# A build-time walk that tries each choice of TensorE in a two-layer attention kernel

## The chip, the cores and the metric

The kernel runs on one core of a Trainium2 chip. The metric is the device time of one execution in microseconds; the time of a version is the median of its runs. A core has five engines that run side by side and meet through semaphores: PE (TensorE; its weight loads are listed as PEld), DVE (VectorE), ACT (ScalarE), POOL (GpSimd) and SP (SyncE, which only issues DMAs here).

## The reference

For each of 16 images of 64 channels by 56 x 56 tokens there are two layers. Layer 0 is windowed cosine attention (8 heads of 8 channels, windows of 7 x 7 tokens) with a group norm, an MLP and a second residual. Layer 1 is full attention over all 3136 tokens:

```
h = _window_cosine_attn(x, qkv_w, qkv_b, logit_scale, bias_table, rel_index, proj_w, proj_b)
h = jax.nn.relu(_group_norm(x + h, gn1_w, gn1_b, GROUPS))
m = _group_norm(h, mlp_gn_w, mlp_gn_b, GROUPS)
m = jax.nn.relu(jnp.einsum('bchw,ec->behw', m, mlp_w1) + mlp_b1[None, :, None, None])
m = jnp.einsum('behw,ce->bchw', m, mlp_w2) + mlp_b2[None, :, None, None]
z = jax.nn.relu(_group_norm(h + m, gn2_w, gn2_b, GROUPS))
...
attn = jax.nn.softmax(jnp.einsum('bhdn,bhdm->bhnm', q, k) * scale, axis=-1)
out = jnp.einsum('bhnm,bhdm->bhdn', attn, v).reshape(b, c, h, w)
return jnp.einsum('oc,bchw->bohw', w_proj, out) + x
```

In layer 1 there are 4 heads of 16 channels. Its softmax subtracts the true maximum of each row, so every score is computed twice: once for the maxima and once for the exponentials.

## The kernel before

**Layer 1 as steps.** An image's attention is 8 stages: 4 heads times 2 halves of the queries. A stage is 25 tiles of 128 keys, and a tile is 4 units of 392 queries, so there are 800 units u = 0 to 799 per image. Unit u has `score` u (one matmul of 392 columns into one of three PSUM banks), then `exp` u on ACT into one of eight buffers, and each fourth unit is followed by `weigh` q, which multiplies the four exponentials of tile q by V in four 32-column tiles of the array. `score` u waits for `exp` u - 3. A `max` step is two matmuls on PE and one maximum over them on DVE; there are 400 per image, 200 for each two heads, and those of a stage must be finished before the stage begins. A `shift` step then moves the negated maxima into three rows of `q_stack` through SP. `copy` and `store` take a stage's result to DRAM.

**Layer 0 as steps.** During the attention of image b the kernel also computes layer 0 of image b + 1: `xload` and `xorder` (x from DRAM, reordered by windows on POOL), `qk`, `sum`, `norms`, `spread`, per window row g the steps `wscore`, `wsum`, `wval`, `wtrans`, `wpv`, `wproj`, then the group norms (`gn`, `affine`, `relu`, `zrelu`), `mlp1` and `mlp2`, and last `gqk`, `gv` and the twelve transfers of each `stack`, which put Q and K of the next image in place. `stack` 3 of an image is issued in the next loop iteration, since head 3 is in use until then. Each half of an image is ended by `sums` (row sums from DRAM), `zload`, `srecip` (DVE), `rden`, `rspread`, `scale` (POOL), `final` (PE and DVE) and `write`.

**Two PSUM slots.** All steps of the list `SLOTS`, that is all but `score` and `weigh`, take turns on two slots of two banks; such a step waits on PE until the one two places before it is emptied by DVE or ACT. DVE, ACT, POOL and SP each take their instructions in program order, so an instruction that waits holds back all behind it.

**The order is written at build time.** `arrange` walks through one image with a clock of its own, in units of 10 ns: `PARTS` is how long each part of a step takes on its engine, `TAIL` how long until others may use it. The engine that is free first takes the offered step of lowest rank. `MORE` is the order of the loop's 15 iterations, `LAST` that of the sixteenth image (no layer 0 beside it), `PROLOGUE` is layer 0 of the first image and `EPILOGUE` the last half's end. These costs only set the order; nothing on the chip waits for them. Three lines on SP matter below; the third is the first thing that `sums` does:

```
                        sp.wait_ge(s_out_copied, b * STAGES + 1)
...
                        sp.wait_ge(s_x_by_windows, t * 8 + g - 1)
...
                    sp.wait_ge(s_out_stored, b * 512 + (64 if half == 1 else 512))
```

The first belongs to `stack` 3, the second to `xload` g from g = 2 on: x_in has two buffers, and POOL must have reordered the earlier one.

## Time and profile before

| | |
|---|---|
| median of 3 runs | 10851.35 us (10829.22 to 10851.8) |
| the profiled execution, its own time | 10812.4 us |
| its span in the trace | 10810.6 us |
| mean granted clock of TensorE | 0.95 |
| PE busy | 9939.2 us (92%) |
| DVE busy | 7775.1 us (72%) |
| ACT busy | 6386.1 us (59%) |

A share of busy time is a mean over the whole span. An idle stretch is listed in the trace in brackets behind the instruction that ended it, with the engine and line that released it. The granted clock has two levels here, 1.2 GHz (0.5) and 2.4 GHz (1.0), so a stretch's mean says what part of it was spent at the lower one.

### The profile page before, as it was taken

The numbers are of one execution on the slowest core, as the hardware profiler recorded it, in microseconds if no ns is written. First come the engines' busy times: TensorE is split into PE (matmuls) and PEld (weight loads), VectorE is DVE, ScalarE is ACT, GpSimd is POOL, SyncE is SP. The second block draws the span as 40 slices with busy tenths as digits, with TensorE's granted clock in tenths as the row PEclk, the third lists the DMA queues.
The fourth block names the chain that finished last, engine by engine and source line by source line (L and its number), as shares of the span: only waits on it lengthen the run. The fifth ranks groups of instructions, "written<-read, shape, count | busy, mean of one in ns | idle before, by whom it ended". The sixth has DMA issues, their size and how long they took to land.

```text
span 10810.6 us, 221389 instructions
## 1 busy us (share of the span) xinstructions
PE 9939.2 (92%) x69254; PEld 3841.5 (36%) x69254; DVE 7775.1 (72%) x10052; ACT 6386.1 (59%) x14066; POOL 972.7 (9%) x834
## 2 busy tenths in 40 slices
PE   5899999999999999999999999999999999999998
PEld 2333433334333333333333333343333433333332
DVE  4676877768677786776767777687776867778675
ACT  1365665656656566565656656566565665656666
POOL 3100101001010000100001010110100101000000
PEclk8799999999999999999999999999999999999999
DMA  0202011020110201111020110201102011020100
GB/s 22 34 5 38 10 19 26 8 36 8 24 22 13 32 7 25 21 20 25 6 33 14 19 25 6 39 8 19 26 8 37 8 25 20 12 33 7 25 14 15
DMA packets 109028, 213.92 MB, mean 20 GB/s; under 512 B 52854, under 2 KB 84534, under 8 KB 107706
## 3 DMA queue, kind: packets, MB, share of 16 engines
q1 hardware_dynamic: 107842, 198.78, 11.5%
q8 instruction: 663, 10.86, 0.4%
q14 instruction: 523, 4.28, 0.1%
HBM read 66.03 MB, written 41.47 MB: 10 GB/s over the span
## 4 chain that ended last, share of the span: by engine, by line
PE 74%; DVE 6%; ACT 6%; DMA 6%; issue 4%; SPq 3%; POOL 1%; ACTq 0%; DVEq 0%; POOLq 0%
PE PS L1219 21%; PE PS L1074 19%; PE PS L1208 16%; DVE small L860 4%; PE PS L1115 3%; ACT exps L796 3%; PE PS L1133 2%; PE PS L1163 2%; PE PS L1171 2%; DMA x_in<-in_x 2%; DMA scratch_rden<-small 2%; PE PS L1123 2%; SPq L592 1%; PE PS L1197 1%; PE PS L1179 1%
## 5 line engine op out<-in xcount | busy, mean ns | idle before, releaser
L796 ACT ACTIVATE exps<-PS 128x392 f32<-128x392 f32 x12800 | 5475.9, 500 | 3683.6 <-PE PS L1208 3655.9
L860 DVE TENSOR_REDUCE small<-PS 128x1 f32<-128x784 f32 x6400 | 5970.6, 968 | 1777.1 <-PE PS L1074 1751.1
L1208 PE MATMUL PS<-q_stack,k_stack 99*128 99x392 bf16 x12800 | 3426.2, 341 | 201.6 <-ACT exps L796 196.3
L1074 PE MATMUL PS<-k_stack,q_stack 96*128 96x392 bf16 x12800 | 3202.9, 342 | 317.0 <-DVE small L860 202.6
L1219 PE MATMUL PS<-exps,v_all 128*32 128x392 f32 x25600 | 2870.8, 521 | 11.9 <-ACT exps L796 9.4
L1208 PEld LDWEIGHTS PS<-q_stack,k_stack 99*128 99x128 bf16 x12800 | 1241.4, 99 | 2077.3 <-ACT exps L796 1156.9
L1074 PEld LDWEIGHTS PS<-k_stack,q_stack 96*128 96x128 bf16 x12800 | 957.5, 99 | 2650.5 <-issue 1217.8
L1219 PEld LDWEIGHTS PS<-exps,v_all 128*32 128x32 f32 x25600 | 510.9, 109 | 800.9 <-issue 582.9
L695 POOL TENSOR_TENSOR win_scores<-win_scores,small 128x784 f32<-128x784 f32 x256 | 383.9, 1500 | 3424.6 <-DVE small L910 3424.6
L1115 PE MATMUL PS<-kmask,tok_unit 113*64 113x392 f32 (+1 forms) x2048 | 398.6, 510 | 33.2 <-DVE small L860 21.3
L753 ACT ACTIVATE win_probs_t<-PS 98x1024 f32<-98x1024 f32 x256 | 262.1, 1024 | 169.7 <-PE PS L1133 167.8
L898 DVE TENSOR_REDUCE small<-PS 128x16 f32<-128x784 f32 x256 | 248.2, 970 | 145.2 <-PE PS L1115 145.2
L1133 PE MATMUL PS<-ident_f,win_scores 128*98 128x128 f32 x2048 | 283.3, 283 | 27.0 <-DVE small L860 21.3
L708 POOL TENSOR_TENSOR att<-att,inv_sums 64x784 f32<-64x784 f32 x66 | 119.8, 1833 | 1814.0 <-DMA inv_sums<-scratch_rden 1814.0
L901 DVE TENSOR_TENSOR win_scores<-PS,small 128x784 f32<-128x784 f32 x256 | 249.5, 975 | 36.8 <-DVE small L898 7.4
L1133 PEld LDWEIGHTS PS<-ident_f,win_scores 128*98 128x98 f32 x2048 | 220.6, 130 | 146.9 <-DVE small L860 124.1
L1197 PE MATMUL PS<-att,w_p 64*64 64x392 f32 x264 | 141.1, 671 | 120.0 <-POOL att L708 120.0
L909 DVE TENSOR_REDUCE small<-win_scores 128x16 f32<-128x784 f32 x256 | 244.5, 955 | 8.8 <-ACT win_scores L748 8.8
L773 ACT ACTIVATE win_scores<-PS,vec 128x392 f32<-128x392 f32 x256 | 136.5, 584 | 192.3 <-PE PS L1163 192.3
L748 ACT ACTIVATE win_scores<-win_scores 128x784 f32<-128x784 f32 x256 | 221.7, 866 | 39.4 <-DVE win_scores L901 38.0
L983 DVE TENSOR_TENSOR inv_sums<-PS,z_half 64x392 f32<-64x392 f32 x132 | 68.0, 552 | 230.4 <-PE PS L1197 230.4
L1123 PE MATMUL PS<-w_v,x_tw 64*98 64x64 f32 x2048 | 208.7, 253 | 9.1 <-DVE win_scores L901 9.1
(102 smaller groups left out, 4151.6 us busy)
## 6 DMA issues: line engine op xcount, KB each, us to landing
q_stack<-tok_qk SPq DMA_DIRECT2D x320, 98.0 KB, 3.7
k_stack<-tok_qk SPq DMA_DIRECT2D x320, 98.0 KB, 4.2
kmask<-tok_unit SPq DMA_DIRECT2D x1024, 12.2 KB
scratch_att<-o_st SPq DMA_DIRECT2D x512, 26.0 KB
att<-scratch_att SPq DMA_DIRECT2D x33, 392.0 KB
z_half<-scratch_z SPq DMA_DIRECT2D x33, 392.0 KB, 11.1
inv_sums<-scratch_rden SPq DMA_DIRECT2D x132, 98.0 KB, 3.3
out<-inv_sums SPq DMA_DIRECT2D x33, 392.0 KB, 3.7
```

The lines of the kernel that those rows point to most:

```text
L695: nc.gpsimd.tensor_tensor(S3, S3, rden[:, 16 * half:16 * half + 16].unsqueeze(2) .broadcast_to([128, 16, WTOK]), ALU.mult).then_inc(s_win_ ...
L753: nc.scalar.activation(win_probs_t[0:2 * WTOK, 2 * half:2 * half + 2, :], PS[0:2 * WTOK, it.bank:it.bank + 2, :], ACT.Copy)\
L796: nc.scalar.activation(exps(u), PS[:, u % SCORE_BANKS, 0:GTOK], ACT.Exp, scale=D1 ** -0.5).then_inc(s_exps, 1)
L860: nc.vector.tensor_reduce(max_parts[:, n_:n_ + 1], slot(), op=ALU.max, axis=AX.XY)\
L901: nc.vector.tensor_tensor(pair(win_scores, half).rearrange("p (a h m) -> p a h m", a=2, m=WTOK), scores, top.unsqueeze(3).broadcast_to([12 ...
L1074: last = mm(PS[:, it.bank + j, 0:GTOK], q_stack[0:STACK, stage // 2, tile * 128:(tile + 1) * 128], k_stack[0:STACK, stage // 2, chunk * GT ...
L1115: last = mm(PS[64 * (w % 2):64 * (w % 2) + m, it.bank + i // 2, 0:GTOK], tok_unit[0:CH + WTOK, q0:q0 + m], kmask[0:CH + WTOK, :, w * WTOK: ...
L1123: last = mm(PS[0:2 * WTOK, it.bank, w * CH:(w + 1) * CH], x_tw[:, w, :, :].rearrange("c a m -> c (a m)"), w_v0[:], start=True, stop=True)
L1133: last = nc.tensor.transpose(PS[0:2 * WTOK, it.bank + p, q * 128:(q + 1) * 128], win_scores[:, c0:c0 + 2 * WTOK], ident_f32[:])
L1197: last = mm(PS[0:CH, it.bank + j, 0:GTOK], w_p1[:], att[:, sl], start=True, stop=True)
L1208: mm(PS[:, u % SCORE_BANKS, 0:GTOK], k_stack[0:STACK + SHIFT, h, kt * 128:(kt + 1) * 128], q_stack[0:STACK + SHIFT, h, c * GTOK:(c + 1) * ...
L1219: last = mm(PS[32 * j:32 * j + 32, PV_BANK, 0:GTOK], v_all[:, stage // 2, kt, :], exps(4 * quad + j), start=(kt == 0), stop=(kt == TILES - 1))
```

## The change

The build-time walk becomes a class `Walk`. Where PE has more than one step to choose from, `arrange` copies the walk, takes one candidate of each kind (`score`, `weigh`, `max`, "layer 0"), runs the copy on for `AHEAD` = 600 units (6 us of the walk's own clock) and keeps the candidate after which PE got most work done. `weigh` has no fixed place among the scores any more: it must only keep its own order, and jumps ahead once 7 scores are out beyond it. `SWITCH` adds 9 units where PE goes from an ordinary step to one in array tiles or back, and the tiled steps' own costs are lowered. `LATE` replaces one constant by a table of how late transfers are counted. `stack` 3 now asks for `sums` 1 first, so it stands behind it on SP. In `earliest_unit`, layer 0's window rows stand 13 quads apart instead of 10, and `final` has no earliest place. No instruction of any engine differs but in its place, apart from the waits on registers that a merged row needs or not.

```
-    "score": (("PE", 17),), "exp": (("ACT", 41),), "weigh": (("PE", 86),),
+    "score": (("PE", 17),), "exp": (("ACT", 41),), "weigh": (("PE", 69),),
...
-STACK_TAIL = 900
+LATE = {"stack": 1200, "xload": 800, "sums": 1500, "zload": 1500, "rden": 600, "rspread": 700}
+AHEAD, PATIENCE = 600, 40
+SWITCH, TILED, URGENT = 9, ("weigh", "sum", "wscore", "wpv"), 7
...
-MAX_START, MAX_RATE = 1, 2.0
+MAX_LOW, MAX_START, MAX_RATE = 4, 6, 2.0
...
-    needs[at("stack", 3)] = []
+    needs[at("stack", 3)] = [(at("sums", 1), None)]
...
-    first, period = 20, 10
+    first, period = 18, 13
...
-    for k in range(2):
-        quad[at("final", 1, k)], quad[at("final", 0, k)] = 8 + k, 185 + k
...
+                behind = self.taken < MAX_LOW + MAX_RATE * self.unit / 4
+                overdue = self.unit > self.pace[n] + PATIENCE if self.pace[n] else False
+                rank = {"shift": 0, "max": 1 if behind else 3}.get(kind, 0 if overdue else 2)
...
+            elif e == 0:
+                if step.i != self.weighed:
+                    continue
+                rank = 0 if self.scored - 4 * self.weighed >= URGENT else 5
...
+        if e == 0:
+            duration += SWITCH * (self.tiled != (kind in TILED))
+            self.tiled = kind in TILED
...
+        if e == 0 and len(found) > 1 and found[0][0]:
+            tried, firsts, until = [], {}, walk.free[0] + AHEAD
+            for _, _, n in found:
+                kind = walk.tasks[n][0].kind
+                firsts.setdefault(kind if kind in ("score", "weigh", "max") or not attended else "layer 0", n)
+            for m, n in enumerate(firsts.values()):
+                other = walk.again()
+                other.take(0, n)
+                tried.append((-min(walk.took[n], AHEAD) - other.work(until), m, n))
+            best = min(tried)[2]
```

The first place is SP at the start of a loop iteration. Before, the twelve transfers of `stack` 3 stand first (`q_stack<-` and `k_stack<-`), then `sums` (`small<-scratch_att` and `att<-`), `zload` and the x loads:

```order
L592 DMA q_stack<-tok_qk 16x3136 x5
L592 DMA q_stack<-piece_l 16x3136
L592 DMA k_stack<-tok_qk 16x3136 x4
L592 DMA k_stack<-piece_l 16x3136
L592 DMA k_stack<-tok_qk 16x3136
L603 ISA
L478 ISA
L605 DMA small<-scratch_att 128x1x49
L607 DMA att<-scratch_att 64x1x1568
```

With the change the same place has `sums`, `zload`, the first four x loads, then `stack` 3, and `rden` (`scratch_rden<-small`) behind it:

```order
L643 DMA x_in<-in_x 64x392
L669 ISA
L677 DMA q_stack<-tok_qk 16x3136 x5
L677 DMA q_stack<-piece_l 16x3136
L677 DMA k_stack<-tok_qk 16x3136 x4
L677 DMA k_stack<-piece_l 16x3136
L677 DMA k_stack<-tok_qk 16x3136
L702 ISA
L703 DMA scratch_rden<-small 128x49
```

So `sums` moved ahead of the twelve stack transfers, and those moved behind the fourth x load, which waits for POOL.

The second place is PE in the same stretch, at the first steps of layer 0. Before, at unit 28, `qk` 1 (`PS<-x_w,w_qk`) is followed by a maximum, two scores and a `weigh` (the ISA rows are its waits):

```order
L1084 ISA
L1060 ISA
L1088 MATMUL PS<-x_w,w_qk 128x392 x2
L1060 ISA
L1074 MATMUL PS<-k_stack,q_stack 128x392 x2
L1207 ISA
L1208 MATMUL PS<-q_stack,k_stack 128x392
L1207 ISA
L1208 MATMUL PS<-q_stack,k_stack 128x392
L1217 ISA
L1219 MATMUL PS<-exps,v_all 32x392 x4
```

With the change `qk` 0, 1 and 2 stand in a row at unit 43:

```order
L1173 MATMUL PS<-x_w,w_qk 128x392 x2
L1169 ISA
L1145 ISA
L1173 MATMUL PS<-x_w,w_qk 128x392 x2
L1169 ISA
L1145 ISA
L1173 MATMUL PS<-x_w,w_qk 128x392 x2
L1292 ISA
L1293 MATMUL PS<-q_stack,k_stack 128x392
```

So the first three `qk` steps have moved from units 24, 28 and 32 to unit 43 and stand next to each other; the two `final` steps follow at unit 47 instead of 32 and 37. On DVE, `srecip` 1 now stands behind sixteen `max` steps of the iteration instead of six. Late in the image `final` 0 moved from units 740 and 745 to 772.

The third place is PE in the steady part of the sixteenth image, where scores (`PS<-q_stack,k_stack`), maxima (`PS<-k_stack,q_stack`) and `weigh` (`PS<-exps,v_all`) are all that is left. Before:

```order
L1219 MATMUL PS<-exps,v_all 32x392 x4
L1074 MATMUL PS<-k_stack,q_stack 128x392 x2
L1208 MATMUL PS<-q_stack,k_stack 128x392 x2
L1074 MATMUL PS<-k_stack,q_stack 128x392 x2
L1208 MATMUL PS<-q_stack,k_stack 128x392 x2
L1219 MATMUL PS<-exps,v_all 32x392 x4
```

With the change:

```order
L1304 MATMUL PS<-exps,v_all 32x392 x4
L1293 MATMUL PS<-q_stack,k_stack 128x392
L1159 MATMUL PS<-k_stack,q_stack 128x392 x2
L1293 MATMUL PS<-q_stack,k_stack 128x392 x2
L1159 MATMUL PS<-k_stack,q_stack 128x392 x2
L1293 MATMUL PS<-q_stack,k_stack 128x392
L1304 MATMUL PS<-exps,v_all 32x392 x4
```

The same work stands between two `weigh` steps, but one score has moved from before a `weigh` to behind it.

## Rows read from the trace of the kernel before

**Rows 1.** The page's part 1: busy time and instructions of each engine

```profile
PE 9939.2 (92%) x69254; PEld 3841.5 (36%) x69254; DVE 7775.1 (72%) x10052; ACT 6386.1 (59%) x14066; POOL 972.7 (9%) x834
```

**Rows 2.** One DVE line of layer 0, once per image (count, first and last start)

```profile
L881 DVE TENSOR_SCALAR tok_h<-PS x15: 566/567/567, 429.6 to 9670.6; 128x392 f32<-128x392 f32 x15
```

**Rows 3.** Windows of one image: length, busy (x instructions) by engine, then PEclk, DMA, GB/s

```profile
3012.00:3069.00 57.00, 46.91 (x224) 15.96 (x221) 31.17 (x36) 22.86 (x49) 14.40 (x15) 0.78 0.43 67
...
3109.00:3149.00 40.00, 38.79 (x334) 17.37 (x327) 31.13 (x38) 26.68 (x58) 5.24 (x4) 1.00 0.05 11
...
3563.00:3594.00 31.00, 30.50 (x211) 11.02 (x209) 25.52 (x34) 21.71 (x52) 0.00 (x0) 1.00 0.01 2
3594.00:3636.00 42.00, 35.89 (x215) 12.09 (x214) 26.46 (x32) 22.07 (x52) 3.62 (x2) 0.88 0.23 43
```

**Rows 4.** Timeline of DVE and PE at an image's start: start, length, [idle before <-releaser]

```profile
3026.03 0.47 DVE L975 RECIPROCAL small<-small 128x49 f32<-128x49 f32 x1 [6.64 <-DMA small<-scratch_att]
...
3027.38 0.83 PE L1074 MATMUL PS<-k_stack,q_stack 96*128 96x392 bf16 x2 [5.66 <-DVE small L860]
...
3038.21 1.58 PE L1088 MATMUL PS<-x_w,w_qk 64*128 64x392 f32 x4 [2.57 <-POOL x_w L673]
```

**Rows 5.** Timeline of SP, same stretch: start and length of issuing

```profile
3008.77 1.26 SPq L544 DMA_DIRECT2D scratch_att<-o_st  x4
...
3023.04 0.61 SPq L605 DMA_DIRECT2D small<-scratch_att  x1
...
3025.79 13.23 SPq L558 DMA_DIRECT2D x_in<-in_x  x4
3039.15 0.51 SPq L618 DMA_DIRECT2D scratch_rden<-small  x1
...
3042.41 1.88 SPq L624 DMA_DIRECT2D inv_sums<-scratch_rden  x4
```

**Rows 6.** Timeline of POOL, same stretch

```profile
3037.07 1.01 POOL L673 COPY x_w<-x_in 64x392 f32<-64x392 f32 x2 [27.67 <-DMA x_in<-in_x]
...
3047.68 3.66 POOL L708 TENSOR_TENSOR att<-att,inv_sums 64x784 f32<-64x784 f32 x2 [2.53 <-DMA inv_sums<-scratch_rden]
```

**Rows 7.** Timeline at the same image's end: SP, then PE

```profile
3594.15 1.25 SPq L544 DMA_DIRECT2D scratch_att<-o_st  x4
3601.21 0.58 SPq L605 DMA_DIRECT2D small<-scratch_att  x1
...
3604.13 0.36 SPq L618 DMA_DIRECT2D scratch_rden<-small  x1
3614.40 1.70 SPq L624 DMA_DIRECT2D inv_sums<-scratch_rden  x4
...
3621.35 2.84 PE L1197 MATMUL PS<-att,w_p 64*64 64x392 f32 x4 [6.07 <-POOL att L708]
```

**Rows 8.** Timeline of PE with four scores, a maximum and a weigh

```profile
2494.21 0.66 PE L1208 MATMUL PS<-q_stack,k_stack 99*128 99x392 bf16 x3
...
2495.13 0.34 PE L1208 MATMUL PS<-q_stack,k_stack 99*128 99x392 bf16 x1
2495.40 0.87 PE L1219 MATMUL PS<-exps,v_all 128*32 128x392 f32 x8
2496.20 0.84 PE L1074 MATMUL PS<-k_stack,q_stack 96*128 96x392 bf16 x4
```

**Rows 9.** Timeline of SP: the first and last issue of two stacks

```profile
3498.36 3.39 SPq L592 DMA_DIRECT2D q_stack<-tok_qk  x5
...
3517.97 0.94 SPq L592 DMA_DIRECT2D k_stack<-tok_qk  x1
```

**Rows 10.** The sixteenth image on PE: at its start and at its last final

```profile
10292.10 0.83 PE L1074 MATMUL PS<-k_stack,q_stack 96*128 96x392 bf16 x2 [8.20 <-DVE small L860]
...
10737.21 5.46 PE L1197 MATMUL PS<-att,w_p 64*64 64x392 f32 x8 [6.39 <-POOL att L708]
```

**Rows 11.** Waits over the whole span: total us, times, longest

```profile
PE PS L1074 <- DVE small L860: 202.6, 325, 8.2
```

More of the change, by code:

```diff
@@ L242, in arrange @@
                 if kind == "max":
[L243 removed]
+                    if self.maxima[self.taken] != step[1:]:
                         continue
[L245 removed]
+                    if self.unit < UNITS - 1 and self.taken > MAX_START + MAX_RATE * self.unit / 4:
                         continue
[L247 to L253 removed]
```

199 lines of the change are left out of this document (124 added, 75 removed).

## The prediction

> **What bounds the kernel now.** I read the page's busy times first. PE is busy for 92% of the span, DVE for 72%, ACT for 59% [rows 1], so the question is how PE's time is filled, and only waits that end on PE count. The second view is one line of layer 0 that runs once per image: its 15 starts lie 14 images apart, (9670.6 - 429.6) / 14 = 660.1 us per image [rows 2]. The third is a table of windows of one image, cut where 50 more units are scored; the table has 16 windows, four are shown [rows 3]. An even window, 3109 to 3149, is 40 us long with 38.8 us of PE at clock 1.00. Two stand out. The first, 3012 to 3069, is 57 us long at a granted clock of 0.78: its 46.9 us of PE would be 46.9 x 0.78 = 36.6 us at the full clock. The other, 3594 to 3636, is 42 us at 0.88, so 35.9 x 0.88 = 31.6 us of work, where the window before it took 31 us. Then I read the timelines of these two for the wait that starts each.
>
> At the start DVE stands 6.64 us at the reciprocal of the row sums until their transfer lands, and PE waits 5.66 us for the maximum behind it; eleven microseconds later PE waits 2.57 us for POOL, which waits for x [rows 4]. SP had sent the twelve transfers of `stack` 3 ahead, so the sums left only at 3023.04 and the first x load at 3025.79 [rows 5]. At the end PE waits 6.07 us for POOL's scaling: SP sent the sums 7.1 us after the store, `rden` needed 10.3 us until 3614.40, and PE could begin 7.0 us after that [rows 7]. After each such wait the clock is at its lower level for a while: 2 x (1 - 0.78) x 57 = 25 us of the first window, 2 x 0.12 x 42 = 10 us of the other [rows 3].
>
> The third thing to see is small and everywhere. Three scores, a maximum and a fourth score: the fourth starts 0.92 us after the first, where the work between is 3 x 0.165 + 0.33 = 0.83 us or less; with four scores in a row it would be 0.50 us [rows 8]. The fourth needs the bank that the exponential of the first empties, so 0.92 us is the least distance of `score` u from u - 3.
>
> **The change part by part.** The work stays: the same matmuls, maxima and exponentials. Everything is a move.
>
> *Start of an image.* The sums cannot leave before the last store has landed. It was issued at 3008.77 [rows 5], and 7.06 us pass at the other such place [rows 7]: 3015.8 instead of 3023.0. `srecip` stands ten maxima later on DVE, at unit 21, some 15 us on, so the 5.66 us go. What is late next is layer 0. The first x load follows the sums by 2.75 us, at 3018.6; before, 11.3 us passed from its issue to POOL's reorder, which takes 1.0 us for two [rows 5, 6], so both are ordered at 3030.9. Only then may SP send the next two x loads and `stack` 3 behind them, 10.3 us of issues (two stacks in 20.5 us [rows 9]), so `rden` leaves at 3042 and x 4 and x 5 a microsecond later. With `rden`'s own 3.3 us [rows 5] as a price for them too, x 5 is ordered at 3047. PE comes to `qk` 0 at unit 43: of the 36.6 us for 50 units [rows 3] I take off seven layer-0 or `final` steps of about 1.5 us (one of them took 1.58 [rows 4]), add five more maxima at 0.34 and take 43/50 of it, 23.9 us, 24.6 with the even window's 3%; 3 us more, my estimate, for the lower clock at the image's start. That is 3039.7. `qk` 0 and 1 fit, `qk` 2 waits from 3042.8 to 3047, 4.3 us. `rspread` goes out 3.3 us after `rden`, scaling starts 5.3 us later and its first half is done after 1.8 us [rows 5, 6]: 3052.4, where PE arrives at 3051. So 8.2 us of wait become about 6, and one spell of low clock of two goes. At half speed, 10 us of it cost 4.5 us. Gain 2.5 + 4.5, and something for `final`: **8 us**. Bounds: 57 - 36.6 x 40 / 38.8 = **19 us** if no wait is left; **3 us** if the moved `stack` 3 delays `qk` 2 and `final` by 5 us more.
>
> A rule bears on this. The row shows 11.3 us for a load of 98 KB [rows 5, 6]. The Trainium skill (DMA: Bandwidth & Descriptors, section on queues, rings and completion order) says that each DMA engine consumes descriptors in ring order. By that the load stands behind `att` and `z_half`, which still precede it, and the 11.3 us stay; if they came from the stack's transfers instead, x 0 would be ready some 8 us sooner and `qk` 2 would hardly wait, 4 us more gain per image. I take the slower reading.
>
> *End of an image.* `final` 0 moves from units 740 and 745 to 772. The sums leave at about unit 711 as before, `srecip` now stands at unit 738, and from `rden` to PE it took 17.2 us [rows 7]. The window 3563 to 3594 had 31 us for 50 units [rows 3], so the 34 units to 772 are 21 us: no wait, by 4 us. The window falls from 42 to 31.6 x 31 / 30.5 = 32 us at best, 10 us; I take **8 us**, bounds 0 and 10.
>
> *Spacing of scores.* Matmuls of scores and maxima start 0.165 us apart: three take 0.66 us and four 0.84 us, the last one's own 0.34 among them; so `score` is 0.165 and `max`, two of them, 0.33. `weigh` to the next start is 0.80, and a score before it 0.27, that is 0.10 more [rows 8]. With these I counted in both orders the scores that stand less than 0.92 us behind the third one before. In `MORE` 131 are short by 21.6 us together, with the change 71 by 8.7 us. In `LAST` it is 197 by 28.3 us and then 50 by 14.5 us. Some of it lies in stretches that wait anyway. **12 us** per image, bounds 6 and 13.
>
> *Waits for maxima elsewhere.* 202.6 us over the span [rows 11], less 5.66 x 15 + 8.2 for the starts, is 109 us or 7 us per image. The walk that looks ahead sees them; new rows of eight `mlp` steps may make others. **3 us**, bounds -4 and 7.
>
> *Switches.* Each costs the 0.10 us above. The order has 417 switches between ordinary and tiled steps, with the change 413: nothing. The Trainium skill (TensorEngine Tiling (Array Packing), section Key Properties) says that a change of tiling mode drains the engine; by it too the sum would move only by these four. This speaks against the weights of the change, not for them.
>
> *The sixteenth image.* Its start wait of 8.20 us goes with 2 us of clock, 10 us; the wait of 6.39 us before the last `final`, whose 8 matmuls ran at half speed [rows 10], goes too, 9 us; spacing 13 us. **32 us**.
>
> Sum: 15 x (8 + 8 + 12 + 3) + 32 = 497 us. From the profiled execution's 10812.4 that is 10315; the median of the runs shown is 39 us above it, so the forecast is **10350 us**, 4.6% faster.
>
> **Rivals.**
> 1. *Waits are truly gone.* The x loads come early and `qk` 2 does not wait: 11 us more per image, 10350 - 165 = 10185. For it: DMA is only partly busy there (0.43 [rows 3]). Against: the 13.2 us that four x loads held SP [rows 5].
> 2. *Half is given back.* PE's waits move to `qk` 2 and `final` 1 (3 us gain at the start), scores stand further apart but then wait for an ACT that is behind after the four `relu` in a row (2 us), maxima nothing: 15 x 13 + 20 = 215, 10635.
> 3. *Nothing changes*: PE's busy 92% is the bound and moved gaps only merge. The clock of 0.78 beside a wait speaks against. 10850.
> 4. *Slower, by one mechanism.* Layer 0 ends about 80 units later, so `stack` 0 to 2 are issued from unit 630 on, and `shift` 7 stands behind all three on SP. Three stacks take 31 us [rows 9]; with 0.62 us per unit [rows 3] they end near unit 675, and the shift is due at 700, 15 us later. Each microsecond beyond is a wait of all of PE. It decides when the stacks end 15 + 31 = 46 us late; at 50 us late it costs 35 per image against 31 won: 10350 + 15 x 35 = 10875, and the low clock behind such a wait (10 us of it, 4.5 us each) makes it 10940.
>
> **How the numbers follow.** My forecast, 10220 to 10480 from start gains of 3 to 15 and the other bounds: 0.50. Rival 1: 0.17. Rival 2: 0.18. Rival 3: 0.05. Rival 4: 0.10. The range 10180 to 10640 reaches from rival 1 to rival 2. The runs shown differ by 0.2%, which is about what a measurement can tell from no change. Faster by over 0.2%: 0.86 (the first three, and a tenth of rival 4), within: 0.05, slower: 0.09.
>
> **What the next profile would show.** Right: no DVE reciprocal behind idle time at an image's start; a PE wait of some 4 us at `qk` 2 and a smaller one at `final` 1; `final` 0 without one; the clock near 0.85 in the first window and 1.00 in the last; the period of the layer-0 line near 629 us. Wrong: a PE wait of over 10 us at `qk` or `final` 1, a `shift` 7 that lands after its stage is due, or a period with the waits gone and still over 645 us, which would mean that PE's own work was longer than I priced it.

## The result, and the profile after

| | before | after |
|---|---|---|
| median of the runs | 10840.28 us (4 runs, 10785.34 to 10851.8) | 10125.55 us (4 runs, 10120.28 to 10143.26) |
| profiled execution, its span | 10812.4 us, 10810.6 us | 10121.69 us, 10119.9 us |
| mean granted clock | 0.950 | 0.968 |

The ratio is 0.9354, 95% interval 0.9327 to 0.938: 6.5% faster. The forecast was 10350 us with a range down to 10180, so the direction is right and the time lies below the range. The spans differ by 690.7 us, where 497 were forecast.

The page after, busy times first (busy us, share of the span, instructions), then the chain that ended last by engine:

```profile
PE 9685.7 (96%) x69254; PEld 3807.6 (38%) x69254; DVE 7762.6 (77%) x10052; ACT 6507.8 (64%) x14066; POOL 974.3 (10%) x834
...
PE 83%; DVE 5%; DMA 4%; SPq 3%; issue 2%; ACT 2%; POOL 1%; DVEq 0%; ACTq 0%; POOLq 0%
```

The instructions are the same in number, and DVE's busy time with them [rows 1]. PE's busy time fell by 253 us although its work stayed: busy time is not work, since a matmul at the lower clock lasts nearly twice as long (eight of one `final` took 5.46 us in [rows 10] and take 2.84 us at the full clock, below).

The line of layer 0 that [rows 2] count, from the second image's call on (count, shortest/median/longest ns, first and last start):

```profile
L966 DVE TENSOR_SCALAR tok_h<-PS x14: 565/566/568, 1040.7 to 9070.6; 128x392 f32<-128x392 f32 x14
```

(9070.6 - 1040.7) / 13 = 617.7 us per image, against 660.1: 42.4 us, where the four terms add up to 31.

Windows of the fifth image, units 0 to 50, 50 to 100, 700 to 750 and 750 to the next image (columns as in [rows 3]); the last line is the same stretch before, units 750 to the next image:

```profile
2832.00:2881.00 49.00, 45.92 (x220) 16.05 (x218) 33.53 (x39) 21.51 (x49) 12.88 (x14) 0.81 0.45 70
2881.00:2927.00 46.00, 44.70 (x257) 16.82 (x257) 31.27 (x39) 25.53 (x55) 2.32 (x2) 0.88 0.06 14
3388.00:3416.00 28.00, 28.00 (x205) 10.66 (x203) 24.15 (x28) 22.30 (x52) 0.00 (x0) 1.00 0.23 50
3416.00:3451.00 35.00, 30.84 (x209) 10.67 (x202) 21.28 (x31) 21.94 (x51) 4.21 (x3) 0.96 0.07 16
```

```profile
3636.00:3672.00 36.00, 31.69 (x201) 11.56 (x198) 25.06 (x33) 21.44 (x51) 0.52 (x1) 0.91 0.08 13
```

The first window is 8 us shorter than before's 57 [rows 3], at a mean clock of 0.81. Units 700 to 750, 42 us at 0.88 before, are 28 us at 1.00, with PE busy all the time. But `final` 0 is no longer among them: its eight matmuls, 2.84 us of work, stand at 3428.03 in the last window, with no wait before them. The fair comparison is units 700 to 800: 42 + 36 = 78 us before, 28 + 35 = 63 us after. The timeline of the same image's start (start, length, idle before and its releaser):

```profile
2836.03 0.59 SPq L690 DMA_DIRECT2D small<-scratch_att  x1
2836.99 0.55 SPq L692 DMA_DIRECT2D att<-scratch_att  x1
2838.09 0.57 SPq L698 DMA_DIRECT2D z_half<-scratch_z  x1
...
2839.10 1.20 SPq L643 DMA_DIRECT2D x_in<-in_x  x2
...
2849.15 0.45 DVE L1060 RECIPROCAL small<-small 128x49 f32<-128x49 f32 x1
...
2849.76 1.03 POOL L758 COPY x_w<-x_in 64x392 f32<-64x392 f32 x2 [20.20 <-DMA x_in<-in_x]
...
2861.90 0.85 SPq L703 DMA_DIRECT2D scratch_rden<-small  x1
...
2867.86 2.62 PE L1173 MATMUL PS<-x_w,w_qk 64*128 64x392 f32 x4 [3.08 <-POOL x_w L758]
...
2874.06 5.49 PE L1282 MATMUL PS<-att,w_p 64*64 64x392 f32 x8
```

The sums leave 4 us after the image's first score, and the reciprocal has nothing to wait for. `rden` stands behind the stack and leaves 25.9 us after the sums. `qk` 2 waits 3.08 us for x, `final` 1 hardly. But the eight matmuls of `final` 1 take 5.49 us: they still run at the lower clock. The bank that `qk` 2 writes comes free late too, for a reason that the prediction did not see: DVE empties it for `qk` 0 into `tok_qk`, and must first wait until `stack` 3, which reads from there, has landed.

```profile
2865.14 1.98 DVE L962 TENSOR_SCALAR tok_qk<-PS,vec 128x784 f32<-128x784 f32 x2 [2.18 <-DMA k_stack<-tok_qk]
```

Two waits of the whole span, after (total us, times, longest), to be read beside [rows 11]:

```profile
PEld PS L1159 <- DVE small L945: 894.1, 1710, 1.3
...
PE PS L1159 <- DVE small L945: 79.6, 239, 0.9
```

and two rows of the weight loads before, which the prediction did not look at:

```profile
PEld PS L1074 <- issue: 1217.8, 1928, 3.9
...
PEld PS L1074 <- DVE small L860: 747.8, 1152, 8.9
```

These rows are idle time of the weight loads alone, and PE can be busy with matmuls meanwhile. Laid over the records of the matmuls, 1175.0 of the 1217.8 us and 545.2 of the 747.8 us lie in time in which PE was busy, and after, 812.6 of the 894.1 us. So the length of such a row is not a wait of PE. What PE itself was idle ahead of scores and of maxima stands behind the second bar in the page's part 5, before and then after:

```profile
L1208 PE MATMUL PS<-q_stack,k_stack 99*128 99x392 bf16 x12800 | 3426.2, 341 | 201.6 <-ACT exps L796 196.3
L1074 PE MATMUL PS<-k_stack,q_stack 96*128 96x392 bf16 x12800 | 3202.9, 342 | 317.0 <-DVE small L860 202.6
```

```profile
L1293 PE MATMUL PS<-q_stack,k_stack 99*128 99x392 bf16 x12800 | 3524.3, 336 | 31.8 <-ACT exps L881 19.3
L1159 PE MATMUL PS<-k_stack,q_stack 96*128 96x392 bf16 x12800 | 3186.0, 338 | 150.8 <-DVE small L945 79.6
```

### The profile page after: what moved, and what is told of

Its sections match the earlier page's. It is cut to its first block, busy times and chain, and to the rows that moved or that the text cites. A ratio compares the mean times of both kernels' runs of the same rounds, so it can differ in the third digit from the quotient of the medians.

```text
span 10119.9 us, 221389 instructions
## 1 busy us (share of the span) xinstructions
PE 9685.7 (96%) x69254; PEld 3807.6 (38%) x69254; DVE 7762.6 (77%) x10052; ACT 6507.8 (64%) x14066; POOL 974.3 (10%) x834
## 4 chain that ended last, share of the span: by engine, by line
PE 83%; DVE 5%; DMA 4%; SPq 3%; issue 2%; ACT 2%; POOL 1%; DVEq 0%; ACTq 0%; POOLq 0%
PE PS L1304 23%; PE PS L1293 21%; PE PS L1159 20%; PE PS L1200 3%; DVE small L945 3%; PE PS L1218 2%; DMA x_in<-in_x 2%; PE PS L1208 2%; PE PS L1248 2%; PE PS L1256 2%; SPq L677 2%; ACT exps L881 1%; PE PS L1282 1%; PE PS L1273 1%; PE PS L1236 1%
## 5 line engine op out<-in xcount | busy, mean ns | idle before, releaser
L881 ACT ACTIVATE exps<-PS 128x392 f32<-128x392 f32 x12800 | 5591.0, 499 | 3029.7 <-PE PS L1293 2919.7
L1293 PE MATMUL PS<-q_stack,k_stack 99*128 99x392 bf16 x12800 | 3524.3, 336 | 31.8 <-ACT exps L881 19.3
L1159 PE MATMUL PS<-k_stack,q_stack 96*128 96x392 bf16 x12800 | 3186.0, 338 | 150.8 <-DVE small L945 79.6
L1304 PE MATMUL PS<-exps,v_all 128*32 128x392 f32 x25600 | 2823.2, 513 | 19.4 <-ACT exps L881 13.2
L1293 PEld LDWEIGHTS PS<-q_stack,k_stack 99*128 99x128 bf16 x12800 | 1200.0, 98 | 2418.8 <-ACT exps L881 1566.3
L1159 PEld LDWEIGHTS PS<-k_stack,q_stack 96*128 96x128 bf16 x12800 | 1049.3, 99 | 1728.4 <-DVE small L945 894.1
L1218 PE MATMUL PS<-ident_f,win_scores 128*98 128x128 f32 x2048 | 277.0, 280 | 18.7 <-DVE small L945 10.7
L793 POOL TENSOR_TENSOR att<-att,inv_sums 64x784 f32<-64x784 f32 x66 | 120.9, 1850 | 1459.0 <-DMA inv_sums<-scratch_rden 1459.0
L1040 DVE SCALAR_TENSOR_TENSOR tok_h<-PS,vec,tok_h 64x392 f32<-64x392 f32 x128 | 79.1, 618 | 212.6 <-PE PS L1256 209.2
L930 DVE BATCH_NORM_STATS2 small<-tok_h 64x6 f32<-64x392 f32 x384 | 208.4, 556 | 9.8 <-ACT tok_h L848 1.1
L1208 PEld LDWEIGHTS PS<-w_v,x_tw 64*98 64x98 f32 x2048 | 192.9, 167 | 49.5 <-DVE win_scores L986 33.4
```

The costliest lines, as they stand in the source:

```text
L881: nc.scalar.activation(exps(u), PS[:, u % SCORE_BANKS, 0:GTOK], ACT.Exp, scale=D1 ** -0.5).then_inc(s_exps, 1)
L1159: last = mm(PS[:, it.bank + j, 0:GTOK], q_stack[0:STACK, stage // 2, tile * 128:(tile + 1) * 128], k_stack[0:STACK, stage // 2, chunk * GT ...
L1208: last = mm(PS[0:2 * WTOK, it.bank, w * CH:(w + 1) * CH], x_tw[:, w, :, :].rearrange("c a m -> c (a m)"), w_v0[:], start=True, stop=True)
L1218: last = nc.tensor.transpose(PS[0:2 * WTOK, it.bank + p, q * 128:(q + 1) * 128], win_scores[:, c0:c0 + 2 * WTOK], ident_f32[:])
L1293: mm(PS[:, u % SCORE_BANKS, 0:GTOK], k_stack[0:STACK + SHIFT, h, kt * 128:(kt + 1) * 128], q_stack[0:STACK + SHIFT, h, c * GTOK:(c + 1) * ...
L1304: last = mm(PS[32 * j:32 * j + 32, PV_BANK, 0:GTOK], v_all[:, stage // 2, kt, :], exps(4 * quad + j), start=(kt == 0), stop=(kt == TILES - 1))
```

## The experiments

All ratios are to the kernel of before, with their 95% intervals. A time "slower than after" is the difference of two ratios at 10840 us, and is known to some 30 to 60 us. Beside the profiles I counted three numbers for each kernel and an average image (the first fifteen): the period, from the records of ACT's exponentials, 800 an image; the time in which the trace's records of granted clock stand at the lower level; and the close scores, counted in the order as the prediction did (how far scores stand below 0.92 us behind the third one before, in sum). The first two are also given by stretch of units:

```
us per image         period  low clock  close   0-100       100-500      500-700      700-800  (low clock)
before                660.5    56.0     21.6   99.3 (28.5)  334.7 ( 2.3)  149.4 (11.2)   77.1 (14.1)
after                 617.5    29.5      8.7   89.2 (18.0)  301.0 ( 0.2)  164.4 ( 9.3)   62.9 ( 1.9)
e12b_ranks_only       661.3    52.5     21.3  101.0 (26.6)  316.6 ( 4.1)  167.3 ( 7.1)   76.5 (14.8)
e10_look_only         654.2    71.4      9.0   96.9 (38.0)  348.3 (19.3)  136.4 ( 3.2)   72.6 (10.9)
e3_not_late           642.0    59.5      9.1   96.4 (36.3)  308.0 ( 0.0)  164.8 ( 9.6)   72.8 (13.6)
e5_not_spread         621.7    36.1      8.0   89.0 (15.6)  332.2 (12.5)  137.8 ( 6.4)   62.7 ( 1.6)
e4_no_look            646.2    40.3     23.7   96.7 (25.0)  315.5 ( 3.9)  168.3 (10.0)   65.7 ( 1.4)
e1_late_only          652.0    51.7     22.4   94.1 (22.9)  337.1 ( 6.6)  153.1 (19.6)   67.6 ( 2.6)
e2_spread_only        669.5    73.7     22.1  102.2 (27.3)  314.1 ( 7.7)  178.0 (30.5)   75.1 ( 8.3)
f1b_before_fill       658.1    48.2     21.6   98.6 (26.2)  335.7 ( 4.3)  150.7 (13.9)   73.1 ( 3.8)
s1_before_short_max   652.7    58.0     21.6   98.5 (26.1)  329.5 ( 5.5)  148.2 (12.7)   76.5 (13.6)
s2_after_short_max    608.2    28.9      8.7   90.3 (21.8)  294.9 ( 0.0)  160.3 ( 5.9)   62.7 ( 1.2)
e6_stack_first        622.7    33.6      8.8   93.5 (19.6)  300.9 ( 0.2)  165.5 (11.8)   62.8 ( 2.0)
e9_max_old            618.6    27.2      8.8   89.8 (22.1)  305.9 ( 0.0)  159.1 ( 4.6)   63.8 ( 0.6)
x_qk_late             622.6    34.1      7.6   86.5 (21.2)  309.5 ( 3.4)  163.7 ( 7.5)   62.7 ( 1.9)
y_sw12                623.4    36.3      7.2   95.7 (23.3)  301.6 ( 0.0)  163.3 (12.3)   62.8 ( 0.7)
yb_20_12              625.4    44.7      6.6   92.1 (22.7)  301.2 ( 1.6)  169.5 (19.3)   62.6 ( 1.1)
yb_ahead400           646.9    73.6      4.8   86.5 (16.4)  315.5 (21.6)  177.8 (29.8)   67.1 ( 5.8)
e7_no_switch          670.9   120.9     10.1   69.6 ( 8.8)  332.9 (35.3)  127.4 ( 9.1)  141.0 (67.8)
f2_after_fill         619.4    30.9      8.7   91.8 (20.7)  300.8 ( 0.0)  164.0 ( 8.4)   62.8 ( 1.8)
```

### The parts of the change, one done and one undone

**e1_late_only**: before, with the late transfers alone.

```diff
-STACK_TAIL = 900
+LATE = {"stack": 1200, "xload": 800, "sums": 1500, "zload": 1500, "rden": 600, "rspread": 700}
...
-    needs[at("stack", 3)] = []
+    needs[at("stack", 3)] = [(at("sums", 1), None)]
...
-    for k in range(2):
-        quad[at("final", 1, k)], quad[at("final", 0, k)] = 8 + k, 185 + k
...
-        end = now + duration + (STACK_TAIL if kind == "stack" else TAIL[engine])
+        end = now + duration + (LATE.get(kind, TAIL[engine]) if attended else 900 if kind == "stack" else TAIL[engine])
```

> The kernel before with the transfers counted late alone (the LATE table, stack 3 behind the sums, no earliest place for final); its old walk, weights and spread stay. Theory A (my terms are right but for the maxima elsewhere): the two waits go, 16 us per image and 19 us in the sixteenth, so about 260 us faster than before, ratio 0.976. Theory B (the low clock behind those waits costs more than I priced): 23 us per image and more, 370 us faster, ratio 0.966 or less. Theory C (what I priced at nothing, layer 0 spread out, is where the rest came from): as A here.

Measured 0.9817 (0.9768 to 0.9867), 198 us: less than either theory had. Its windows for units 0 to 50, 50 to 100 and 700 to 750:

```profile
2959.00:2989.00 30.00, 30.00 (x194) 10.80 (x192) 23.21 (x27) 20.96 (x51) 2.08 (x4) 0.92 0.57 83
2989.00:3052.00 63.00, 55.26 (x284) 20.23 (x276) 38.66 (x50) 25.62 (x56) 16.07 (x14) 0.86 0.12 25
3538.00:3567.00 29.00, 29.00 (x201) 10.62 (x203) 24.11 (x28) 20.98 (x51) 0.00 (x0) 1.00 0.23 49
```

The end is won: units 700 to 800 take 67.6 us in place of 77.1. The start is won in part, 99.3 to 94.1 us: the three quads of `qk` stand at unit 50, and the waits meet again in the second window, 63 us with 7.7 us of PE idle and a clock of 0.86.

**e2_spread_only**: before, with layer 0 spread alone (`first, period = 18, 13`).

> The kernel of before with nothing but layer 0 spread (first work at unit 72 and 52 units from group to group, in place of 80 and 40). Theory A (the parts help one another): by itself, under the old walk with its fixed final sums and stacks ahead, it is worth little, 0 to 40 us, ratio 0.996 to 1.0. Theory C (spreading is worth the same everywhere): 50 to 90 us, ratio 0.992 to 0.995.

Measured 1.0055 (1.0027 to 1.0084): slower, which neither theory had. The window of units 600 to 650, with before's own for comparison:

```profile
3544.00:3597.00 53.00, 48.09 (x269) 19.11 (x267) 29.24 (x37) 31.56 (x63) 8.13 (x7) 0.87 0.37 52
```

```profile
3532.00:3562.00 30.00, 29.76 (x207) 10.69 (x205) 25.28 (x29) 21.13 (x51) 0.52 (x1) 1.00 0.37 46
```

The old walk puts layer 0's end there as one cluster, with DVE busy for only 29.24 of 53 us: few maxima among the steps. 25.9 of the 30.5 us of low clock in units 500 to 700 lie in this window.

**e3_not_late**: after, with the late transfers taken back (the diff of e1 in the other direction).

> The change with the transfers counted as before and stack 3 first again; lookahead, free weigh and spread stay. Theory A: it keeps 12 us for spacing and 9 for maxima per image, 15 x 21 + 13 = 330 us faster than before, ratio 0.97. Theory B: only what is left of 6.46% after 370 us, about 340 us, 0.969 too, but the low clock at an image's start and end as before. Theory C: the same total with the gain lying in the layer-0 windows.

Measured 0.9682 (0.9632 to 0.9732): both theories had this total, so it doesn't tell them apart. **e4_no_look**: after, without the look ahead.

```diff
-            if e == 0 and len(found) > 1 and found[0][0]:
+            if False:
```

> The change without the lookahead: at each choice the lowest rank is taken. The count of short scores in its order is 153 by 23.7 us against 71 by 8.7 us. Theory A: spacing 15 us and the maxima waits 6 us per image come back, 15 x 21 + 15 = 330 us slower than the change, ratio to before 0.966. Theory B: only the spacing, 240 us slower, 0.957. Theory C: as B.

Measured 0.9773 (0.9725 to 0.9821), 454 us more than after by the ratios, more than either theory expected. The close scores alone went from 8.7 to 23.7 us; PE's idle time ahead of scores and maxima, 31.8 and 150.8 us in after, went up as well:

```profile
L1293 PE MATMUL PS<-q_stack,k_stack 99*128 99x392 bf16 x12800 | 3436.0, 337 | 157.7 <-ACT exps L881 152.6
L1159 PE MATMUL PS<-k_stack,q_stack 96*128 96x392 bf16 x12800 | 3165.6, 339 | 239.3 <-DVE small L945 166.5
```

**e5_not_spread**: after, with `first, period = 20, 10`.

> The change with layer 0's rows 10 quads apart from quad 20 again, all else as changed. Theory A and B: the same as the change within 3 us per image, ratio to before 0.935 to 0.940. Theory C (DVE and ACT are more evenly loaded when layer 0 is spread): 10 us per image are lost, 150 us slower than the change, ratio 0.949.

Measured 0.9411 (0.9366 to 0.9456): 62 us slower than after, nearer to theories A and B (45 us at most) than to C (150 us). **e10_look_only**: after with e3's and e5's edits together. **e12b_ranks_only**: the same without the look ahead, e4's edit too.

> The new walk (it looks ahead, its ranks and maxima rules are those of after), with neither the late transfers (stack 3 ahead of the sums again, one constant for all stacks, final sums at their old fixed places) nor the spread layer 0. In the order its close scores are 68 by 9.0 us an image (before 131 by 21.6, after 71 by 8.7). Theory A (each part gives its own share, whatever the others do): the walk gives what taking it out of after cost, less what e4 still held, 250 to 300 us beside what its spacing alone predicts (190 us): ratio 0.972 to 0.977. Theory B (the walk gives spacing and shorter waits for maxima, some 22 us an image, and the waits at start and end stay): 320 to 370 us, ratio 0.966 to 0.970, and low clock time stays at 1000 to 1150 us. Theory C (the parts help one another so far that the walk alone is worth less than its spacing): under 190 us, ratio 0.983 or more.

> The new walk's ranks and rules for maxima, but with no look ahead, no late transfers and no spread layer 0: the corner from which e10 and e4 are each a step or two away. Close scores 143 by 21.3 us an image (before 131 by 21.6). Theory A (the parts help one another mainly through low clock time): this is within 60 us of before, ratio 0.995 to 1.005, so that the look ahead alone (e10) is worth 130 to 200 us here against 469 in after. Theory C (the ranks do a large part of it): 100 us or more faster than before, ratio 0.991 or less.

e10: 0.9846 (0.982 to 0.9873), theory C; e12b: 1.0002 (0.9983 to 1.002), theory A. With these the parts can be compared alone and beside the others (ratios differ by these amounts, at 10840 us). Late transfers alone and spreading alone were run on the old walk and not on the new ranks, so two corners of a full set are missing:

- the ranks alone: nothing;
- the look ahead: 169 us on the ranks alone (e12b to e10), 454 on late and spread (e4 to after);
- late transfers: 198 us on before (e1), 472 on the look ahead (e10 to e5), 356 with spread too (e3 to after);
- spreading: -60 us on before (e2), 178 on the look ahead (e10 to e3), 62 with late too (e5 to after).

Alone they are worth 198 - 60 + 169 = 307 us, together 700. Without the look ahead, late and spread together are worth 248 us on the ranks (e12b to e4), so most of what is more than a sum comes with the look ahead. The table shows what the look ahead alone was missing: close scores fall from 21.3 to 9.0 us, and low clock rises from 52.5 to 71.4 us an image. Its first window:

```profile
2982.00:3046.00 64.00, 53.59 (x227) 17.54 (x224) 32.78 (x38) 22.20 (x51) 14.40 (x15) 0.73 0.37 60
```

64 us at 0.73, worse than before's 57 at 0.78 [rows 3]. A walk that fills PE's gaps leaves the waits for transfers where they are, and between these PE was at the lower clock for longer. With the transfers counted late (e5) low clock falls to 36.1, spread too (after) to 29.5.

### Is it the maxima, and is it the clock?

**s1_before_short_max** and **s2_after_short_max**: DVE takes the maxima over a quarter of the columns and leaves out the rest of that work, in both orders.

```diff
-                    nc.vector.tensor_reduce(max_parts[:, n_:n_ + 1], slot(), op=ALU.max, axis=AX.XY)\
+                    nc.vector.tensor_reduce(max_parts[:, n_:n_ + 1], slot(98), op=ALU.max, axis=AX.XY)\
```

> The kernel of before, except that VectorE takes every maximum of the global scores over 98 of their 392 columns (so the softmax's shift is that of a quarter of the scores: work left out of the maxima). VectorE then has each block of maxima done some 0.2 us earlier, and TensorE's scores for a maximum should hardly wait for it; the order of all instructions is that of before. Theory A (the waits for maxima are what the prediction mis-sized): TensorE's waits on VectorE in the before order cost more than the 202.6 us on its own row, since the waits of its weight loads are a part of them; this kernel is then 250 to 350 us faster than before, ratio 0.968 to 0.977. Theory B (those waits were sized right, and the rest of the gain is low clock behind waits for transfers): only about 120 to 190 us faster, ratio 0.982 to 0.989.

> The kernel of after with the same short maxima (98 of 392 columns; work left out of the maxima). What it gains on after is what waits on maxima still cost in the new order. Theory A: the new order has taken most of them away, so that this one gains 60 to 150 us on after (ratio to before 0.920 to 0.929), and the difference between the two gains is what the new order won on maxima: 150 to 200 us, where the prediction had 45. Theory B: both gains are nearly the same, differing by 45 us or less.

Measured 0.9861 (0.9817 to 0.9905), 151 us on before, and 0.9195 (0.9156 to 0.9234), 172 us on after. A maximum took 360 ns in place of 967:

```profile
L945 DVE TENSOR_REDUCE small<-PS 128x1 f32<-128x196 f32 x6400 | 2280.8, 360 | 4014.8 <-PE PS L1159 3972.4 <-issue 3.3
```

Theory A falls: 151 us where it had 250 to 350, and the two gains are alike, so the new order didn't win 150 us by taking away waits on DVE's speed. What DVE's speed costs, 8 to 9 us an image in the table, it costs in both. That the waits for maxima were therefore sized right, as theory B words it, does not follow: by the second count of the section on the prediction, the time lost ahead of maxima falls from 11.8 (s1) to 6.1 us an image (s2) with short maxima, much as with full ones (21.0 to 15.6).

**f1b_before_fill**: before, with nine matmuls more in the wait ahead of `final` 0.

```diff
                     free()
+                    if half == 0 and k == 0 and 0 < len(before):
+                        for _ in range(9):
+                            mm(PS[:, it.bank, 0:256], w_1[:, 0:128], w_1[:], start=True, stop=True)
                     wait_apart(pe, s_att_scaled, finish(half, b) * 2 + k + 1)
```

> The kernel of before with work added: ahead of each image's first final sum of half 0 TensorE runs nine more matmuls of 64 x 256 on constant weights, into the bank that this sum overwrites (work added; the output is the same). They take some 4 us and stand where TensorE waited 5.3 us for GpSimd's scaled rows, then worked on at a low granted clock (11.5 us of low clock in this stretch of 41.1 us). Theory B (half the price of a wait is the low clock behind it): with TensorE busy in the wait the clock stays up, and the stretch loses 3 to 6 us: 45 to 90 us faster in all, though work was added. Theory A (a wait costs its own length): nothing gained, 0 to 15 us slower.

Measured 0.9961 (0.9937 to 0.9985): 42 us faster with more work, interval 16 to 68, and theory B had 45 to 90. The place in the timeline, and its window:

```profile
3609.25 4.15 PE L1196 MATMUL PS<-w 64*128 64x256 f32 x18
3614.52 1.50 PE L1200 MATMUL PS<-att,w_p 64*64 64x392 f32 x4 [1.11 <-POOL att L708]
```

```profile
3586.00:3623.00 37.00, 35.88 (x226) 14.49 (x228) 25.60 (x32) 21.26 (x51) 3.63 (x2) 1.00 0.20 41
```

PE still waits for the same scaled rows, 1.11 us after the added work. But the window stays at 1.00 where it had 0.88, the final sum takes 1.50 us where it took 2.84 [rows 7], and units 700 to 750 are 3.6 us shorter (41.1 to 37.5 us on average) with 9.7 us less of low clock. That is the price of the clock by itself: 0.37 us for each of its microseconds here, on top of the wait. Theory B holds at this place.

**f2_after_fill**: the same idea in after, five such matmuls ahead of the third quad of `qk`.

> The kernel of after with work added: ahead of each image's third quad of qk TensorE runs five more matmuls of 64 x 256 on constant weights (some 2.4 us), where it waits 3.1 us on the average for GpSimd's tokens in order of windows, with 14.7 us of low clock in the image's first stretch. If the clock behind that wait is what costs (as in f1b), this stretch loses 1 to 2 us an image and the kernel is 15 to 30 us faster than after; if the wait is short in many images, the added work stands in the way: 0 to 20 us slower.

Measured 0.9353 (0.9326 to 0.9381), as after. Low clock didn't fall (30.9 us). The wait at `qk` 2 is there in 14 of after's 15 images, but the added matmuls do not stand in it: they write the bank that DVE empties behind `stack` 3, and PE waits for that bank first, 2.3 us on average in 14 images:

```profile
2879.75 1.98 DVE L962 TENSOR_SCALAR tok_qk<-PS,vec 128x784 f32<-128x784 f32 x2 [3.51 <-DMA k_stack<-tok_qk]
...
2880.84 3.70 PE L1172 MATMUL PS<-w 64*128 64x256 f32 x10 [2.79 <-DVE tok_qk L962]
```

x is in order about a microsecond after they begin, so they hold `qk` 2 back for the rest of their 3.70 us. In f1b the bank was free when the wait began. So this run doesn't test whether filling that wait would pay.

### Orders around that of after

**e6_stack_first**: after, with `needs[at("stack", 3)] = []` again.

> The kernel of after, with one rule taken back: stack 3 may be issued without waiting for the issue of the sums' transfer, and stands ahead of it in SP's queue again. In the order, the quads of qk then move from units 11, 20, 29 and 38 or so to 23, 31, 42 and 51, and the sums of weights are reached later. Theory A: the start of an image loses what stack 3 ahead costs in the rows of before (11 us of its transfer, of which some 4 to 6 us stand in TensorE's way): 60 to 90 us slower than after. Theory B (a wait for a transfer costs its length again in low clock): 120 us slower than after or more.

Measured 0.9424 (0.9382 to 0.9467), 76 us slower than after as theory A said, most of it in units 0 to 100 (89.2 to 93.5 us).

**e9_max_old**: `MAX_LOW, MAX_START = 0, 1` for `4, 6`.

> After with the old allowance for maxima: none of them is ranked ahead of other work when behind (0 in place of 4), and at most 1 in place of 6 may be ahead at the start of an image. The order keeps few close scores (63 by 8.8 us) but has 432 switches in place of 414 and its quads of qk some 8 units later. Theory A (maxima that come early and in pairs with other work are what shortens the waits on VectorE): waits of TensorE on VectorE's maxima rise by 4 to 6 us an image, 60 to 100 us slower than after. Theory B (the spacing alone does it): within 25 us of after, apart from 27 us for 18 more switches an image at 0.10 us.

Measured 0.9361 (0.9341 to 0.9381), the same as after: theory B, these two numbers do nothing that can be seen.

**x_qk_late**: `quad[at("qk", i)] = 11 + 2 * i` for `6 + i`.

> After, with qk quad i not before unit 4 x (11 + 2i) in place of 4 x (6 + i): the quads are at units 43, 51, 59 and 67 in place of 43, 43, 43 and 52. In after, three quads of qk stand in one place and quad 2 waits for its transfer in half of the images. Theory A: the wait of 3.1 us in half of the images and the cluster with the final sums behind it are gone, 20 to 60 us faster than after. Theory B (the copies of each quad on VectorE and GpSimd then come late for the stacks' users): no gain, or up to 20 us slower.

Measured 0.9391 (0.9371 to 0.941), 40 us slower. Units 0 to 100 do gain 2.7 us, and 100 to 500 lose 8.5: theory B's direction at twice its size. Its reason was not tested.

**e7_no_switch**: `SWITCH = 0` for `9`.

> After with the walk's cost of a switch between the two kinds of matmul set to 0 in place of 9. The order then has layer 0's last work at unit 722 in place of 615, the copies for the next image behind it, and shift 0 at unit 799 in place of 781: the late stacks and the late shift 0 of the prediction's slower rival. Close scores 47 by 10.1 us an image. Theory A (the rival's mechanism holds from here on): stacks 0 to 2 land after the next image's first score, 5 to 15 us of waits an image at the boundary, 75 to 250 us slower than after. Theory B (the transfers still land in time): 15 to 30 us slower than after by the spacing (1.4 us an image), no new wait row on a stack.

Measured 1.0104 (1.0081 to 1.0127): 1.0% slower than before, some 810 us slower than after, and far from both theories. The windows of units 700 to 750 and from there to the next image, and the timeline in the second:

```profile
3636.00:3710.00 74.00, 70.33 (x277) 31.20 (x276) 22.67 (x36) 37.57 (x75) 12.22 (x10) 0.77 0.44 65
3710.00:3776.00 66.00, 55.80 (x273) 15.45 (x274) 55.47 (x66) 21.80 (x49) 0.52 (x1) 0.75 0.17 25
```

```profile
3749.24 16.21 DVE L945 TENSOR_REDUCE small<-PS 128x1 f32<-128x784 f32 x17
...
3750.27 1.72 PE L1159 MATMUL PS<-k_stack,q_stack 96*128 96x392 bf16 x4 [0.19 <-DVE small L945]
3752.17 1.72 PE L1159 MATMUL PS<-k_stack,q_stack 96*128 96x392 bf16 x4 [0.19 <-DVE small L945]
3754.07 1.71 PE L1159 MATMUL PS<-k_stack,q_stack 96*128 96x392 bf16 x4 [0.19 <-DVE small L945]
```

Layer 0 ends at unit 722. The maxima of the next image's first stage need it, so all of them stand behind it: DVE is busy for 22.67 us of the first 74, and then takes 17 maxima in a row while PE runs nothing but their matmuls, a pair of maxima every 1.90 us at the lower clock. The prediction's rival 4 had the late end of layer 0 and looked for its price at late stacks. The price is real, but it is the maxima that come late.

**yb_20_12** (`first, period = 20, 12`), **yb_ahead400** (`AHEAD = 400`), **y_sw12** (`SWITCH = 12`): three orders with fewer close scores than after, tried to beat it.

> After with layer 0's first work at unit 80 and 48 units from group to group (after: 72 and 52). Its order has close scores 61 by 6.6 us an image (after 71 by 8.7) and layer 0's last work at unit 593 in place of 615. Theory A (period = 584 us + 0.8 x low clock time + 1.26 x close scores, fitted over the eleven kernels run so far): 25 to 50 us faster than after unless the low clock time rises. Theory B (the distance of the groups by itself is what helps): as after, within 20 us.

> After with a look 400 ahead in place of 600. The order has the fewest close scores of all (31 by 4.8 us), but layer 0's last work at unit 648 and shift 0 at unit 797, the third quad of qk at 51. Theory A (low clock and close scores set the time): if the low clock time stays at 30 us, 70 to 80 us faster than after. Theory B (layer 0's end late is what made the kernel without a switch cost slow, 870 us): 30 to 200 us slower than after, with low clock time in the last stretches before the next image.

> After with the walk's cost of a switch at 12 in place of 9. Of the orders tried on paper this one is nearest to after's (qk at units 43, 43, 43, shift 0 at 781, layer 0's last work at 612), with close scores 61 by 7.2 us in place of 71 by 8.7. By the close scores alone: 1.9 us an image, 25 to 30 us faster than after. If the low clock time moves, as it did in the two orders before, by 0.8 of it: plus or minus 20 to 180 us; which of the two decides is the question.

Measured 0.9451 (0.9415 to 0.9487), 0.9803 (0.9766 to 0.984) and 0.941 (0.9383 to 0.9436): all slower than after, by 105, 487 and 61 us. In each the low clock time rose, to 44.7, 73.6 and 36.3 us. The fit that the expectation states, period = 584 + 0.80 x low clock + 1.26 x close scores, gives 628.1, 648.9 and 622.1 us for them, measured 625.4, 646.9 and 623.4. It misses e12b by 8.5 us, f1b by 8.3 and e7, where DVE holds up the end of an image, by 23. So it holds for orders near these, and its 0.80 counts the waits that go with the low clock; the clock alone was 0.37 in f1b. No order run here beats after.

## Why the prediction was wrong

The mechanism was right in the main, and the sum too small. Per image, 43.0 us were won (660.5 to 617.5) and 31 forecast. To split them I took each step's distance to the next in both traces, less the tenth percentile of its kind; what is left is put down to low clock stretches, or outside these to what comes next: 

```
us per image beyond the shortest    low clock   before a maximum   before a score   other
before                                37.8            18.9              17.6         26.4
after                                 18.6             9.6               4.6         26.4
```

The split depends on what counts as a kind. Counted again, with steps grouped by kind and by whether one in array tiles comes next, the low clock falls by the same and the other shares move:

```
before                                37.8            21.0              27.7         25.7
after                                 18.7            15.6              12.5         25.7
```

Maxima and scores together fell by 22.3 us in the first count and 20.6 in the second, where the prediction had 3 + 12 = 15. That much holds either way; how it divides does not.

- **Start of an image**: 8 us forecast. Units 0 to 100 fell by 10.1 us, with some 1.5 of close scores in it: right. The sums left early, the reciprocal's wait is gone, `qk` 2 waits 3.1 us on average (4.3 forecast) and `final` 1 little. The first x load took 10.7 us from its issue to POOL again (2839.10 to 2849.76), now with no stack ahead of it and only `att` and `z_half` before it. By the ring order that the Trainium skill states (DMA: Bandwidth & Descriptors, section on queues, rings and completion order) it stands behind these two, and the trace agrees: the reading that I took. The fifth load, issued at 2863.06 right behind the stack, took only 3.6 us to POOL (2866.70), so it was not the stack that made the first one slow.
- **End of an image**: 8 us forecast with 10 as the bound. Units 700 to 800 fell by 14.2 us; 2.4 of it is work that moved to other units and some 1.5 close scores, which leaves 10. The window went to 28 us at 1.00, below the 32 that I called the best, since that 32 still counted the work of `final` 0, which has moved out of it. I took 8 for no reason that a row gave: the low clock behind the wait went with it, as f1b shows (9.7 us of it, 3.6 us of time).
- **Spacing of scores**: 12 forecast; 13.0 in the first count, 15.2 in the second. Right, or a little small.
- **Waits for maxima elsewhere**: 3 us forecast, bounds -4 and 7; measured 18.9 to 9.6, 9.3 us, and 5.4 in the second count. This is the step that failed, and it failed in how it read the row. [Rows 11] give one releaser's part, 202.6 us, of the 317.0 us that PE was idle before a maximum, and idle time is not all: such a matmul is listed as 0.34 us long, while the next can start 0.165 us after it [rows 8], so a wait shorter than the difference does not show. Of the 21.0 us an image of the second count only 12.3 stand in the trace as idle time of PE. So my 7 us were no bound. The rows of the weight loads are none either: of the 1217.8 us behind "issue" 1175.0 lie in time in which PE was busy, and with maxima at 360 ns (s1) the row is still 1185.1. What the 5 to 9 us are is shown in part: not DVE's speed, since shorter maxima gain alike in both orders (151 and 172 us), and the second count falls by 5.7 us with them too (11.8 to 6.1), but where the maxima stand. The second count, done for the other orders too, gives 27.6 us with the ranks alone and 21.2 with the look ahead added (e12b, e10), and 23.3 without it and 15.6 with it beside the other parts (e4, after). That it is the bank of two maxima before, free earlier when they are further apart, is argued from the walk's rule and not shown.
- **The sixteenth image**: 32 forecast, 44.0 measured (534.5 to 490.5 us from its first exponential to the end). Its first 100 units gave 17.0 where I had 10, its last 150 gave 12.4 where I had 9, the rest 14.6 where I had 13. [Rows 10] show the two waits, 8.20 and 6.39 us, and I added 2 and 3 us of clock. The last `final` of half 0 now has no wait and its eight matmuls take 2.84 us instead of 5.46:

```profile
10068.79 2.84 PE L1282 MATMUL PS<-att,w_p 64*64 64x392 f32 x8
```

- **Switches**: nothing, and nothing is seen; the walk's number for them is another thing. At 0 the order is another one, 810 us slower (e7).

So by the first count 6.3 us an image are the maxima, 2 the end, 1 the spacing, 0.6 the start, and the remaining 2 of the 12 stay open; by the second it is 2.4 for the maxima and 3.2 for the spacing, with some 4 open. And the range: all four terms at their own upper bounds (19, 10, 13 and 7 us) are 18 us an image more than the sum, 10350 - 15 x 18 = 10080, and the measured time lies above that. The range's lower end (10180) assumed only one more thing going well. That the parts of the edit help one another, 307 us alone and 700 together, says that a price for one part would not have carried over; the terms of the sum are not these parts, so it does not say which term was off.

## What to carry to other kernels

Where an engine's clock falls behind its waits, price a wait by the window (length, busy time and granted clock before and after), not by its own row; a wait filled with useless matmuls tells what the clock costs, if what they write is free before the wait begins. Idle time before a kind of step is no bound on its waits, since short ones hide in the listed length of a matmul; the distance from start to start shows them. Idle time of the weight loads is no price at all until it is laid over the time in which the matmuls were busy. When several edits take away waits that stand close to one another, try them together too: here late transfers were worth 198 us on the old walk and 472 beside the look ahead, and the look ahead 169 us alone and 454 beside the other two.

## What the hardware showed that I had not expected

- Adding 4.15 us of matmuls per image in front of a wait made the kernel of before 0.4% faster (0.15% to 0.63%): the granted clock of that window was 1.00 in place of 0.88.
- The order of the same 221389 instructions moves the time of an image from 617.5 (after) to 670.9 us (e7), and its low clock time from 27.2 (e9) to 120.9 us (e7).
- With maxima in a row and nothing between, a pair takes 1.90 us: 0.95 for each on DVE, with PE's four matmuls stretched to 1.72 us at the lower clock, where four in mixed work took 0.84 [rows 8].
